# A language-model tower on one core: score products that wait for their banks alone, rounding scalars on VectorE, value sums from a column of ones, and new orders

## The reference

```python
qk = jnp.einsum('bhnd,bhmd->bhnm', q * SCALE, k)
attn = jax.nn.relu(1 + qk + qk * qk / 2)
attn = attn / jnp.sum(attn, axis=-1, keepdims=True)
out = jnp.einsum('bhnm,bhmd->bhnd', attn, v)      # then w_proj, b_proj
```

```python
x_norm = rmsnorm(x, g)
scale = 127.0 / jnp.maximum(jnp.max(jnp.abs(x_norm), axis=-1, keepdims=True), EPS_Q)
x_q = jnp.clip(jnp.round(x_norm * scale), -128, 127) / scale
```

## Time and profile before

| what | us |
|---|---|
| median of three runs (392.15 to 394.27) | 393.11 |
| the profiled execution | 396.22 |
| its span, first to last instruction | 394.2 |
| TensorE busy | 325.8 |
| VectorE busy | 294.0 |
| ScalarE busy | 272.4 |
| GpSimd busy | 235.3 |
| mean granted TensorE clock | 0.908 of full |

### The profile page before, as it was taken

How to read it: one execution, slowest core, us unless ns; L and a number is a source line. 1 busy time by engine, 2 the same in 40 slices (tenths; PEclk the granted TensorE clock), 3 DMA queues, 4 the chain that set the end, 5 groups by cost and what they waited for, 6 DMA issues and landing times. The chain is left out here.

```text
span 394.2 us, 6391 instructions
## 1 busy us (share of the span) xinstructions
PE 325.8 (83%) x1794; PEld 188.7 (48%) x1794; DVE 294.0 (75%) x636; ACT 272.4 (69%) x552; POOL 235.3 (60%) x316
## 2 busy tenths in 40 slices
PE   0199965768978899998989889988998899899955
PEld 0143422254425534364335558646765646477633
DVE  3019999899899899999998959941365737467874
ACT  2459999696688998799876964353555547566852
POOL 6751168578819459296392691760134836678893
PEclk9999995959899998998979969998999969899976
DMA  6891000000000000000000000000000000000111
GB/s 151 150 274 23 1 2 0 2 1 0 2 1 1 2 0 2 2 1 0 2 1 0 1 3 2 0 2 2 0 2 2 0 2 1 2 12 10 32 60 50
DMA packets 7134, 7.87 MB, mean 20 GB/s; under 512 B 1643, under 2 KB 6138, under 8 KB 7098
## 3 DMA queue, kind: packets, MB, share of 16 engines
q1 hardware_dynamic: 5464, 5.71, 4.9%
q0 software_dynamic: 768, 1.57, 2.8%
q10 hardware_dynamic: 866, 0.17, 0.2%
HBM read 5.87 MB, written 1.57 MB: 19 GB/s over the span
## 5 line engine op out<-in xcount | busy, mean ns | idle before, releaser
L983 PE MATMUL bank<-ring,win 128*128 128x512 f32 x96 | 53.4, 690 | 7.4 <-DVE dmin L2248 3.3
L1856 POOL TENSOR_TENSOR arena<-arena 128x512 f32<-128x512 f32 x24 | 34.0, 1428 | 39.9 <-DVE arena L2282 25.9
L2239 DVE SCALAR_TENSOR_TENSOR pair<-bank,cw,pair 128x508 f32<-128x508 f32 (+2 forms) x72 | 49.8, 733 | 5.8 <-issue 4.7
L1838 POOL TENSOR_TENSOR arena<-arena,dl 128x512 f32<-128x512 f32 x24 | 31.9, 1332 | 22.9 <-DVE dl L2231 22.6
L1065 PE MATMUL bank<-wout,pair 128*128 128x192 f32 x192 | 37.7, 352 | 3.3 <-ACT ring L382 3.3
L480 ACT ACTIVATE du<-bank 128x512 f32<-128x512 f32 x48 | 25.3, 597 | 19.9 <-PE bank L1115 17.4
L1065 PEld LDWEIGHTS bank<-wout,pair 128*128 128x128 f32 x192 | 34.1, 206 | 9.5 <-ACT ring L382 3.7
L1844 POOL TENSOR_TENSOR du<-dl,pair 128x512 f32<-128x512 f32 x24 | 33.1, 1383 | 8.8 <-DVE dmin L2248 8.8
L983 PEld LDWEIGHTS bank<-ring,win 128*128 128x128 f32 x96 | 19.0, 216 | 35.0 <-issue 18.8
L2269 DVE TENSOR_TENSOR_SCAN arena<-arena 128x512 f32<-128x512 f32 x24 | 34.8, 1461 | 0.3
L972 PE MATMUL bank<-ident,ring 128*128 128x128 f32 x64 | 11.7, 330 | 23.8 <-ACT ring L409 19.0
(11 more groups left out here) (177 smaller groups left out, 887.1 us busy)
## 6 DMA issues: line engine op xcount, KB each, us to landing
out<-h SPq DMA_DIRECT2D x16, 96.0 KB, 1.6
win<-in_w SPq DMA_DIRECT2D x2, 384.0 KB
arena<-ffn_in_t SPq DMA_DIRECT2D x1, 768.0 KB
wout<-out_w SPq DMA_DIRECT2D x2, 288.0 KB
win_rest<-in_w SPq DMA_DIRECT2D x2, 192.0 KB
arena<-ffn_out_t SPq DMA_DIRECT2D x1, 384.0 KB
wa<-w_qkv SPq DMA_DIRECT2D x1, 384.0 KB
h<-emb,idx POOLq DMA_INDIRECT x16
```

What stands on the lines that cost most here:

```text
L983: nc.tensor.matmul(bank[:, IN_BANKS[j][m], :], win[:, j // NG, m * P:(m + 1) * P], xtr[:, j % 2, i, :], start=True, stop=False)
L1838: nc.gpsimd.tensor_tensor(relu_s[:, c, :], relu_s[:, c, :], dl[:, j % NG, c, :], ALU.subtract).then_inc(rest_done, 1)
L1856: nc.gpsimd.tensor_tensor(yv[:, c, :], yv[:, c, :], bx[:, c, :], ALU.add).then_inc(yv_done, 1)
L2239: nc.vector.scalar_tensor_tensor(acc, seqs(bank[:, IN_BANKS[j][c], :])[:, :, 0:LEN - tap], cw[:, j // NG, c, TAPS - 1 - tap:TAPS - tap], a ...
```

## The change

- `scores(s)` on TensorE no longer waits for `sq_ready`, the squares of all sequences before. The waits for its banks stand in TensorE's list.
- `sq` gets a 129th column of ones for each head, set once by GpSimd (`ones_scores`), and `values(s)` multiplies 129 columns: the last one is the sum of the values over all keys.
- `take_sums(s)` moves from ScalarE to VectorE, where three `tensor_scalar` instructions add that sum, read from PSUM as a scalar of each partition. `turn_sums(s)` is then three transposes, with no ones product.
- The variance, most and step scalars of both roundings move from GpSimd to VectorE: `input_variance`, `input_most`, `input_step`, `hidden_variance`, `hidden_most`, `hidden_step`. The two powers and `gain` stay on GpSimd.
- `project_v` splits its loop in two, with one start and one stop for a bank. `take_v` waits for `pv_ready` instead of `nm_turned`. `square_scores` waits for one chunk more, because `sq` is larger.
- The bank tables and the lists of all engines are new.

```diff
-        SQ = CH * JH * P
+        SQ = CH * JH * (P + 1)
...
             def square_scores(s):
                 if s < 2:
-                    act.wait_ge(scan_dve, (5 + s) * DECAYING * DVE_U)
-                    act.wait_ge(t_ready, CI * (5 + s))
-                    act.wait_ge(bx_ready, CI * (5 + s))
+                    act.wait_ge(scan_dve, (6 + s) * DECAYING * DVE_U)
+                    act.wait_ge(t_ready, CI * (6 + s))
+                    act.wait_ge(bx_ready, CI * (6 + s))
...
-            def take_sums(s):
-                if s == 0:
-                    act.wait_ge(wx_ready, 5)
-                if s >= 2:
-                    act.wait_ge(nm_turned, s - 1)
-                act.wait_ge(pv_ready, CH * s + CH)
-                nc.scalar.activation(nm[:, s % 2, :, :], bank[:, PV_BANKS[s], 0:CH * P].rearrange("p (c n) -> p c n", n=P),
-                                     ACT.Copy).then_inc(nm_out, 1)
...
                 pe.wait_ge(q_out, 4 * g + 4)
                 pe.wait_ge(k_out, 2 * g + 2)
-                pe.wait_ge(sq_ready, CH * s)
...
             def values(s):
                 b, i = seat(s)
                 pe.wait_ge(ones_col, 2 * min(s // SG + 1, 2))
+                pe.wait_ge(ones_sq, 2)
                 pe.wait_ge(v_out, 2 * (s // SG) + 2)
                 for c in range(CH):
                     pe.wait_ge(sq_ready, CH * s + c + 1)
                     for j in range(JH):
-                        last = nc.tensor.matmul(bank[j * HS:(j + 1) * HS, PV_BANKS[s], c * P:(c + 1) * P],
+                        last = nc.tensor.matmul(bank[j * HS:(j + 1) * HS, PV_BANKS[s], c * (P + 1):(c + 1) * (P + 1)],
                                                 va[b][:, i, c * JH + j, :], sq[s % 2][:, c, j, :],
                                                 start=True, stop=True)
                     last.then_inc(pv_ready, 1)
 
             def turn_sums(s):
-                b, i = seat(s)
                 pe.wait_ge(nm_out, s + 1)
-                nc.tensor.matmul(bank[:, SUM_BANKS[s], 0:CH * P], ones[:, :], va[b][:, i, :, :].rearrange("p h w -> p (h w)"),
-                                 start=True, stop=False)
                 for c in range(CH):
-                    last = nc.tensor.matmul(bank[:, SUM_BANKS[s], c * P:(c + 1) * P], nm[:, s % 2, c, :], ident[:, :],
-                                            start=False, stop=(c == CH - 1))
+                    last = nc.tensor.transpose(bank[:, SUM_BANKS[s], c * P:(c + 1) * P], nm[:, s % 2, c, :], ident[:, :])
                 last.then_inc(nm_turned, 1)
...
+            def ones_scores():
+                pool.wait_ge(scan_dve, 7 * DECAYING * DVE_U)
+                pool.wait_ge(t_ready, CI * 7)
+                pool.wait_ge(bx_ready, CI * 7)
+                for b in range(2):
+                    nc.gpsimd.memset(sq[b][:, :, :, P:P + 1], 1.0).then_inc(ones_sq, 1)
...
+            def take_sums(s):
+                if s == 0:
+                    dve.wait_ge(wx_ready, 5)
+                if s >= 2:
+                    dve.wait_ge(nm_turned, s - 1)
+                dve.wait_ge(pv_ready, CH * s + CH)
+                for c in range(CH):
+                    at = c * (P + 1)
+                    last = nc.vector.tensor_scalar(nm[:, s % 2, c, :], bank[:, PV_BANKS[s], at:at + P],
+                                                   bank[:, PV_BANKS[s], at + P:at + P + 1], None, ALU.add)
+                last.then_inc(nm_out, 1)
...
+            def hidden_step(s):
+                dve.wait_ge(inv2_ready, s + 1)
+                nc.vector.tensor_scalar(step2[:, s:s + 1], inv2[:, s, 1:2], QMAX, None, ALU.mult).then_inc(step2_ready, 1)
+                nc.vector.tensor_scalar(deq2[:, s:s + 1], most2[:, s, 1:2], inv2[:, s, 0:1], wmean[:, 1:2], ALU.mult,
+                                        ALU.mult).then_inc(deq2_ready, 1)
```

More of the change, by code:

```diff
@@ new lines, in _ @@
+            pe.wait_ge(attn_ready, 2)
+            project(1)
+            pe.wait_ge(nm_out, 3)
+            turn_sums(2)
+            pe.wait_ge(h_att, 1)
+            pe.wait_ge(x_out, 4)
+            project_qk(1, 0)
+            pe.wait_ge(h_added, 14)
+            project_v(1)
+            pe.wait_ge(q_out, 6)
+            pe.wait_ge(k_out, 3)
+            project_qk(1, 1)
+            pe.wait_ge(nm_out, 4)
+            turn_sums(3)
+            pe.wait_ge(attn_ready, 3)
+            turn_attention(2)
@@ L1541, in _ @@
-            turn_attention(5)
+            turn_sums(5)
+            pe.wait_ge(h_att, 4)
+            values(6)
+            pe.wait_ge(qxt_ready, 1)
+            turn_attention(4)
+            pe.wait_ge(attn_ready, 6)
+            project_up(0, 1)
+            pe.wait_ge(sq_ready, 24)
+            turn_attention(5)
+            project_up(0, 0)
+            pe.wait_ge(att_out, 5)
+            project(4)
+            pe.wait_ge(att_out, 6)
+            project(5)
+            pe.wait_ge(nm_out, 7)
@@ new lines, in _ @@
+            values(7)
+            pe.wait_ge(sq_ready, 27)
+            scores(10)
+            pe.wait_ge(nm_out, 8)
+            values(8)
+            pe.wait_ge(sq_ready, 30)
+            values(9)
+            turn_attention(6)
+            turn_sums(7)
+            project_up(1, 1)
+            pe.wait_ge(nm_out, 9)
+            project_up(1, 0)
+            pe.wait_ge(att_out, 7)
+            turn_sums(8)
+            pe.wait_ge(attn_ready, 8)
+            turn_attention(7)
+            pe.wait_ge(sq_ready, 33)
@@ L1647, in _ @@
[L1647 to L1659 removed]
+            pe.wait_ge(h_att, 9)
+            project_qk(3, 0)
+            pe.wait_ge(qxt_ready, 6)
@@ L1660, in _ @@
+            project_v(3)
+            pe.wait_ge(k_out, 8)
+            pe.wait_ge(q_out, 16)
+            scores(12)
+            pe.wait_ge(attn_ready, 12)
+            pe.wait_ge(y_done, 5)
+            pe.wait_ge(qxt_ready, 7)
             scores(13)
             pe.wait_ge(v_out, 8)
+            project_up(5, 0)
+            turn_hidden(1)
+            pe.wait_ge(sq_ready, 39)
+            project_down(0)
+            turn_attention(11)
+            values(12)
+            pe.wait_ge(sq_ready, 42)
@@ new lines, in _ @@
+            divide(9)
+            round_input(4)
+            input_gain(6)
+            divide(10)
+            input_inverse(5)
+            largest_hidden(1)
+            largest_input(6)
+            hidden_step(0)
+            hidden_most(1)
+            add_attention(7)
+            input_step(5)
+            round_input(5)
+            input_variance(6)
+            hidden_inverse(1)
+            hidden(2)
+            input_stats(7)
+            input_most(6)
+            input_inverse(6)
@@ new lines, in _ @@
+            add_attention(8)
+            hidden_variance(2)
+            input_gain(7)
+            input_stats(8)
+            largest_input(7)
+            input_variance(7)
+            hidden_step(1)
+            input_step(6)
+            hidden(3)
+            add_attention(9)
+            take_sums(11)
+            input_most(7)
+            round_input(6)
+            round_hidden(0)
+            input_inverse(7)
+            input_variance(8)
+            input_gain(8)
+            hidden_variance(3)
```

2306 lines of the change are left out of this document (1121 added, 1185 removed).

## The result

The changed kernel takes **378.61 us** in the median (377.34 to 381.09, 4 runs) against 393.15 for the kernel before, run beside it: ratio 0.9637, 95% interval 0.9581 to 0.9693. The ratios leave out an execution that took over 1.5% longer than the fastest of its kernel, which happened to two of the ten of one experiment, the filled hole. The forecast was 374 us in a range of 363 to 391. The profiled execution took 377.34 us with a span of 375.5 and a mean granted clock of 0.930 (before: 396.22, 394.2, 0.908).

The account below looks back on a forecast made before the run. VectorE was taken to bound the recurrent layers, TensorE attention and feed-forward, and chain latency the drain. Stage -17, drain -3, recurrent stage +1 gave -19 us, from a median of 393.11 to 374 us, range 363 to 391.

Parts of the forecast that it names:

- the stage: Attention and feed-forward, 250 to 380 us: from 130 to 113 us, -17 us, with TensorE and VectorE both nearly full.
- The wait of the score products: TensorE's score products (L1115) waiting for ScalarE's squares, 250 to 380 us: removing the wait closes 0 to 8.7 us idle.
- TensorE's work: 250 to 380 us: no ones product (11.3), transposes for identity products (4.1), extra column (0.1): 15.3 us less, lower bound 11.2.
- VectorE's prices: Instructions moved to VectorE: 0.26 us per value-sum instruction, 0.115 per rounding scalar (0.08 to 0.157); 10 and 14 us in the stage.
- The recurrent stage: The two recurrent layers, up to the last scan: sums added to VectorE, one divide removed, +1 us.
- the drain: Last 14 us, a chain's latency: queueing behind others' scalars on GpSimd goes, -3 us (0 to -5).
- The holes only move: Rival: values wait for squares, VectorE's fuller queue delays TensorE; only removed work counts, part lost: 382 us, chance 0.18.
- VectorE bound: Rival: VectorE becomes the stage's bound and is badly fed, so slower: 399 us at 80% busy, chance 0.14.
- The clock falls: Rival: fewer products bring TensorE's granted clock in the stage from 0.95 to 0.84: 389 us, chance 0.06.

Follow-up runs that it names:

- the filled hole: Kernel before, wait kept, with nine useless score products issued ahead of it for the second sequence of each pair: 389.63 us, ratio 0.9896.

## Why the prediction was right, and where only its total was

The time lies in the range and the stage's total came out, but not by the prediction's own terms: the term that I priced at 8.7 us at most carries nearly all of the gain, and the term of 15.3 us carries none on the old orders. That the two errors cancel is luck.

The 374 us is 4.6 too low, and 4.3 of these have a source of their own. I took the change of a profiled execution, 396.2 to 377.2 us, and set it off the median. The profiled pair did just that (396.22 to 377.34); it lies at the far ends of its two kernels' executions, and the medians are 14.5 us apart.

**The wait of the score products: the step that was mis-sized.** I let it be worth 0 to 8.7 us, read from five idle times. Alone it is worth 19 us of the median, and put back into the changed kernel it takes 15 (14 by the ratios). Three things were missed. The window began at 250 us, so the hole at 228 us and the slow products behind it were left out (4.9). An idle time in the list is shorter than the delay, 1.74 for 1.91 us. And products behind a hole ran at a low clock (6.5 us); the clock of 0.73 in the earlier trace rows was in my hands, but I used it only for a rival, and never as something that closing the holes would give back. The mechanism itself was right: on the old orders no other wait of TensorE grew from 250 to 360 us when it was taken away.

**TensorE's work: forecast -15.3 us in the stage, 18.8 in all.** By total it fell by 13.7 us with the wait kept and 11.1 without. The ones product and the transposes' second record were each priced by their own group, and such groups overlap one another: with the sums alone the groups fell by 19.1 us (7.1 + 6.7 + 13.9 to 8.6) and the total by 13.7. Turned sums do leave 48 records, as forecast. The total of 305.0 us near the forecast 307 is one error covering the other: a part of the fall came from the clock (12.4 us in the kernel without the wait). And less work was worth nothing on the old orders. That a TensorE busy 91% of the stage is its bound, so that less work there shortens it, failed on those orders: its work shrank, and it waited for VectorE and ScalarE instead. In the new orders the old sums, put back, cost 10 to 12 us; how much of that is TensorE's work, and how much ScalarE's copies in a list not made for them, the runs don't tell.

**The stage: forecast -17, measured -16.3, for another reason.** The wait alone does -16.4 on the old orders.

**VectorE's prices held.** Three instructions of the value sums start 0.27 us apart (forecast 0.26), and the sums alone raised VectorE's total by 12.2 us (forecast 12.5). The groups by form, from 250 us to the end, of the sums and of the scalars on the input's side:

```profile
L2274 DVE TENSOR_SCALAR arena<-bank 128x128 f32<-128x128 f32 x42 | 12.1, 345 | 4.0 <-PE bank L1104 4.0
...
L2340 DVE TENSOR_SCALAR deq<-most,inv,wmean 128x1 f32<-128x1 f32 x16 | 4.2, 264 | 0.0
L2330 DVE TENSOR_SCALAR most<-most,amax 128x1 f32<-128x1 f32 x16 | 3.3, 204 | 0.1
L2339 DVE TENSOR_SCALAR step<-inv 128x1 f32<-128x1 f32 x16 | 2.3, 144 | 0.0
L2324 DVE TENSOR_SCALAR ms<-mv 128x1 f32<-128x1 f32 x16 | 2.3, 143 | 0.0
```

Two of the four kinds last longer than my bound of 0.157 us; they overlap with the next instruction, and the total of 13.1 us for 128 (0.102 each) lies within the 0.08 to 0.157. Where VectorE was full, before the last flag, the sums delayed the flag by 1.4 us; in the stage behind, where it had stood idle for 41% of the time, nothing that these runs can tell. By the Trainium skill ("VectorE: DVE Perf Modes", section on the TRN2 errata) I had estimated 258 ns for one of the sums. The 0.27 us from start to start agree; the single instruction lasts 345 ns, well over the table's figure.

**The recurrent stage: forecast +1, measured -1.2; the drain: -3, measured -1.2.** The first is two effects that I had as one: the wait gives 4.9 us back there, and the rest of the change takes 3.7 of them (the sums on VectorE alone +2.5 with the wait kept). The drain was to shrink because the queueing behind the scalars on GpSimd goes. That step failed: moving the scalars alone left it at 13.3 us for 13.2, and putting them back into the changed kernel at 12.2 for 12.0. Where the 1.2 us come from stays open, and they are within what one execution differs from another.

**The rivals.** "The holes only move" has nearest the measured number, 382, and is half true: the holes at the score products did not come back at the value products, but TensorE's shorter list found new waits for VectorE. "VectorE bound" is true in part and without its price: from 228 to 250 us it is busy 21.5 of 22, the stage holds 89%, and at the end of the stage it is full. There TensorE falls to 5.5 busy us of 9, and the clock behind is at its lower level:

```profile
345.00:354.00 9.00, 5.52 (x39) 3.51 (x40) 8.97 (x36) 5.88 (x14) 4.91 (x7) 1.00 0.10 33
354.00:361.00 7.00, 5.88 (x22) 3.18 (x22) 7.00 (x23) 2.51 (x6) 4.42 (x6) 0.50 0.09 28
```

"The clock falls" went the other way over the stage as a whole, 0.97 for 0.95. The Trainium skill's rule that transposes do not count as TensorE's activity ("TensorE: Matmul & The Clock Gate", Part 4) shows nowhere here: with the new sums in place of the ones product and without the wait the clock was 1.00 from 250 to 345 us. The one low stretch that the new sums bring (0.84 from 228 to 250 us) has the 2.49 us of idle TensorE in it, so it speaks for neither. No run has a stretch of transposes alone.

**The best kernel** of the study is the one before with a single line changed, 375.4 us (with the scalars moved as well, 375.76, the same). By the medians the change as made carries 3 us more; on the old orders it is the value sums that bring them.

## What to carry to other kernels

An idle time in a list of waits is not what the wait costs. Here 8.7 us stood for 19; where something else comes late next, it can be worth less than it shows. So look at the granted clock just behind each hole and price the slow products with it, and for the same wait outside the stage that you study. When a change has several parts, a total that comes out proves none of them; run each part alone and take each one back, since here one line did all of it and a part with 13.7 us less work was worth nothing. Work taken from an engine that is 91% busy pays only if what feeds it can deliver sooner, and work moved to another must not land in the stretch in which that one is full.

## What the hardware showed that was not expected

VectorE's rounding of a 128x512 tile, from SBUF to SBUF, took 480 ns in the mean before and 695 ns in the changed kernel, with single ones of 1.50 us. The timelines of VectorE and of GpSimd in the drain of the changed kernel:

```profile
364.50 1.50 DVE L2387 TENSOR_SCALAR pair<-pair,step 128x512 f32<-128x512 f32 x1
```

```profile
364.45 1.26 POOL L1849 TENSOR_TENSOR pair<-pair,gout 128x512 f32<-128x512 f32 x1 [2.73 <-PE bank L1147]
```

The long one starts 0.05 us after GpSimd's gain and ends 0.28 us behind it. With that gain cut to 32 columns, the same group, first in the changed kernel, then with the cut:

```profile
L2387 DVE TENSOR_SCALAR pair<-pair,step 128x512 f32<-128x512 f32 x16 | 11.1, 695 | 0.0
```

```profile
L2387 DVE TENSOR_SCALAR pair<-pair,step 128x512 f32<-128x512 f32 x16 | 7.6, 478 | 0.0
```

478 ns, as before: 3.5 us in this line, and the input's rounding falls too, from 470 to 313 ns in the mean.

The traces show more than a slowdown. Five of the sixteen roundings of the changed kernel start while a gain runs, 0.05 to 0.74 us after its start. They last 0.81 to 1.50 us, but each ends 0.28 us after the end of its gain, whenever it began. So such a rounding stands still until the gain is done. It goes the other way too. With the scalars alone moved on the old orders three gains start inside a rounding; there the rounding keeps its 0.47 to 0.48 us, and the gain lasts 1.38 to 1.55 us for its usual 1.27 and ends 1.13 us after the rounding each time. One of them, VectorE, then GpSimd:

```profile
380.38 0.47 DVE L2363 TENSOR_SCALAR pair<-pair,step 128x512 f32<-128x512 f32 x1
```

```profile
380.43 1.55 POOL L1877 TENSOR_TENSOR pair<-pair,gout 128x512 f32<-128x512 f32 x1
```

The one that starts first goes on and the other waits for it. VectorE's instructions that read PSUM, such as hidden (L2356, 0.74 us), last the same beside a gain.

TensorE can be held up by it: the longest wait in the changed kernel's list is for an input rounding that lasted 1.20 us beside a gain, for 0.31 without one. VectorE, GpSimd and TensorE there:

```profile
344.13 1.20 DVE L2345 TENSOR_SCALAR ring<-ring,step 128x192 f32<-128x192 f32 x1
```

```profile
343.70 1.52 POOL L1849 TENSOR_TENSOR pair<-pair,gout 128x512 f32<-128x512 f32 x1
```

```profile
345.48 0.39 PE L1133 MATMUL bank<-ident,ring 128*96 128x128 f32 x2 [1.59 <-DVE ring L2345]
```

In the kernel before, the longest of the sixteen roundings of hidden values took 490 ns. I first put the long ones down to the scalars, since without them the rounding no longer waits for GpSimd. That does not hold: with the scalars moved on the old orders, with the wait and without, the longest took 481 and 482 ns; with the wait alone taken away one took 820, and with the scalars put back in the changed kernel one still took 1543 ns. It is the order of the two lists that lets a rounding start inside a gain, and the new orders do it more often. What it costs in the end was not tried by itself: the cut gain also shortens the chain through GpSimd, so how much of its 7 us is the price of this stays open.
